# A decoder layer on one core: attention scores computed twice, the first batch in plain fp32, loads on two queues

## The reference

```python
q = silu(x @ Wq1 @ Wq2);  a = exp(log_sigmoid(sigmoid(x @ Wk1 @ Wk2)));  v = x @ Wv      # 512 channels
h[t] = a[t] * h[t-1] + (1 - a[t]) * v[t]                                                 # scan over tokens
x = layernorm(x + (rmsnorm(q * h) * norm_w) @ Wo)
# cross attention, 8 heads of 32 rows: a head is 32 rows of x and 32 rows of ctx
qk = einsum('bdm,bdn->bmn', xh, ctxh) / sqrt(32);  sm = softmax(qk, axis=-1)
x = layernorm(x + einsum('bmn,bcn->bcm', sm, ctxh))
x = layernorm(x + (silu(x @ w_gate.T) * (x @ w_up.T)) @ w_down.T)                         # hidden size 1024
```

## Time and profile before

| | us |
|---|---|
| median of 3 runs | 172.75 (172.38 to 174.07) |
| profiled execution, whole | 172.81 |
| its span on the core | 171.0 |
| PE, PEld busy | 154.1, 142.0 |
| DVE, ACT, POOL busy | 117.2, 111.9, 79.6 |
| shares of the chain that ended last | PE 70%, POOL 10%, issue 4%, ACT 4%, DMA 4%, DVE 3% |

### The profile page before, as it was taken

One profiled execution on the slowest core, in us unless ns is written; L12 is line 12 of the kernel. 1 busy time (PEld: TensorE's weight loads), 2 busy tenths in 40 slices (PEclk: granted clock), 3 DMA queues, 4 the chain that ended last, 5 costly groups with the idle time before them and its releaser, 6 DMA issues.

```text
span 171.0 us, 4005 instructions
## 1 busy us (share of the span) xinstructions
PE 154.1 (90%) x1528; PEld 142.0 (83%) x1528; DVE 117.2 (69%) x214; ACT 111.9 (65%) x258; POOL 79.6 (47%) x95
## 2 busy tenths in 40 slices
PE   7999784599987999999999999999999999899950
PEld 2799674498985899999799999979999979799940
DVE  2568887945987949786795779849749086536642
ACT  3697999859999878299776764854738860124400
POOL 1219999968975384225067123735100455016301
PEclk9999999569999999999999999999999999999995
DMA  5999960100002200000010000100020000000011
GB/s 162 312 395 402 401 230 7 59 4 0 4 0 61 67 0 4 0 0 4 2 61 4 0 6 0 61 4 0 0 64 1 2 4 0 0 0 4 0 61 61
DMA packets 5138, 10.47 MB, mean 61 GB/s; under 512 B 640, under 2 KB 1664, under 8 KB 5120
## 3 DMA queue, kind: packets, MB, share of 16 engines
q1 hardware_dynamic: 5120, 10.23, 17.1%
HBM read 9.18 MB, written 1.05 MB: 60 GB/s over the span
## 4 chain that ended last, share of the span: by engine, by line
PE 70%; POOL 10%; issue 4%; ACT 4%; DMA 4%; DVE 3%; SPq 2%; POOLq 0%; DVEq 0%; ACTq 0%
PE banks L379 38%; PE banks L523 9%; PE banks L463 7%; PE banks L529 4%; PE banks L485 4%; PE banks L450 4%; DMA ctx_raw<-ctx 4%; ACT numer L631 2%; POOL ctx_h_lo L889 2%; POOL xt_lo L923 1%; POOL w_gate_lo L907 1%; POOL o_lo L914 1%; PE banks L473 1%; PE banks L425 1%; PE banks L495 1%
## 5 line engine op out<-in xcount | busy, mean ns | idle before, releaser
L956 POOL TENSOR_TENSOR g_lo<-gu,g_hi 128x512 fp32r<-128x512 f32 x15 | 19.9, 1337 | 34.4 <-ACT g_hi L673 34.4
L631 ACT ACTIVATE numer<-banks,neg_top 128x256 f32<-128x256 f32 x64 | 29.5, 482 | 6.6 <-DVE neg_top L804 6.4
L804 DVE TENSOR_REDUCE neg_top<-banks 128x4 f32<-128x1024 f32 x16 | 19.1, 1217 | 12.0 <-PE banks L450 12.0
L665 ACT ACTIVATE gu<-banks 128x512 f32<-128x512 f32 x16 | 9.6, 598 | 19.4 <-PE banks L379 18.0
L836 DVE SCALAR_TENSOR_TENSOR gu<-gu,banks 128x512 f32<-128x512 f32 x16 | 10.9, 680 | 13.2 <-ACT gu L665 13.2
L642 ACT ACTIVATE prob<-banks 128x1024 f32<-128x1024 f32 x16 | 15.7, 1022 | 4.5 <-PE banks L463 4.4
L937 POOL TENSOR_SCALAR ve<-mv 128x2 f32<-128x2 f32 x12 | 2.3, 193 | 31.0 <-DVE mv L769 30.9
L523 PE MATMUL banks<-w_down_hi,g_hi 128*128 128x256 f32 x64 | 16.0, 284 | 0.0
L775 DVE TENSOR_SCALAR res<-banks,mv,rstd 128x256 f32<-128x256 f32 x24 | 11.9, 536 | 5.9 <-POOL rstd L939 5.8
L463 PE MATMUL banks<-ident,numer 128*128 128x128 f32 x128 | 15.8, 273 | 0.1
L523 PE MATMUL banks<-w_down_lo,g_hi 128*128 128x256 f32 x64 | 15.7, 279 | 0.0
(11 more groups left out here) (111 smaller groups left out, 456.2 us busy)
## 6 DMA issues: line engine op xcount, KB each, us to landing
prob<-w_ffn SPq DMA_DIRECT2D x4, 512.0 KB, 11.6
res<-xT SPq DMA_DIRECT2D x4, 256.0 KB, 5.5
ctx_raw<-ctx SPq DMA_DIRECT2D x4, 256.0 KB, 6.9
ctx_t<-ctxT SPq DMA_DIRECT2D x4, 256.0 KB, 4.9
res<-x SPq DMA_DIRECT2D x4, 256.0 KB, 6.4
...
```

The costliest lines, as they stand in the source:

```text
L631: ins = nc.scalar.activation(numer[:, n % 2, 2 * h + c, :], place["scores", b, i][:, 2 * h + c, :], ACT.Exp, bias=neg_top[:, 2 * i + h, c: ...
L665: nc.scalar.activation(gu[:, n % 2, :].rearrange("p (k t) -> p k t", k=2), place["hidden", b, i][:, 0:2, :], ACT.Tanh, scale=0.5).then_inc ...
L804: nc.vector.tensor_reduce(neg_top[:, 2 * i:2 * i + 2, :].rearrange("p h c -> p (h c)"), place["scores", b, i][:, :, :], AX_X, ALU.max, neg ...
L956: nc.gpsimd.tensor_tensor(g[1][:, 2 * i:2 * i + 2, :], gu[:, n % 2, :].rearrange("p (k t) -> p k t", k=2), g[0][:, 2 * i:2 * i + 2, :], AL ...
```

## The change

Six things change.

1. **Scores made twice.** The first `scores` serve the maximum alone. The maxima are rounded to fp32r, a high part and a rest next to each other (`split_top`, DVE), turned by two 128-column products for a row tile (`turn_top`) and copied by ACT (`keep_top`). PE then makes the scores again with the operands changed over, so that they come out turned, and adds the negated maxima with one more product for each head and piece (`shifted`, with `pick`). One exp of 1024 elements for two heads writes `prob` straight away (ACT). The row sums come from products with ones (`sums`, shaped as `context`), and DVE turns, inverts and spreads them with its own 32 by 32 transposes (`invert`). `turn_exp`, `inverse`, `widen` and the accumulator reads are gone. The factor of the scores moves from x1 into the exp.
2. **The first batch unsplit.** For batch 0 (`WHOLE = 1`) low, value, decay, query, mixed and both passes of scores multiply plain fp32 operands, one matmul in place of three (`whole`). x, low, the outputs, x1 and ctx of batch 0 are not split. The weights still are, for batches 1 to 3. Since the raw weights are read by batch 0, the loads that overwrite them wait for those products.
3. **Two queues.** ACT issues the loads of w_v and of the first xT, in this order, before its first activation; SP issues the others, w_high for decay and w_low first.
4. `norm1` and `norm2` are applied by ACT (a scale and a bias; POOL works out the bias with two more small steps). `norm3` stays on DVE.
5. Gate and up of a `hidden` step lie in banks of their own, each freed by its own reader.
6. The last batch's `down`, `add_down`, `norm3` and store go by halves of 128 rows, and `down` waits for both parts of the last g before its last eight and four products.

Both tables are new. There are three warm-up products in place of four.

```diff
-WARM_UP = 4
+WARM_UP = 3
 ATT_SCALE = float(D) ** -0.5
+WHOLE = 1
...
-    "sp.w_high": [[2.2, 2.7]],
...
+    "sp.w_high": [[0.7, 4.7]],
...
+    "act.load_w_v": [[0.7]],
+    "act.load_xt": [[1.2]],
...
-    "down": [[5], [0], [2], [3]],
...
+    "turn_top": [[3, 2], [0, 0], [0, 3], [4, 6]],
...
+                    "squares": [sq_turned], "mixed": [normed[0]], "sums": [sums_turned], "context": [normed[1]],
                     "turn_x": [x2_lo]}
         place, before, held = {}, {}, {}
...
             def load_ffn(c):
                 if c >= 2:
                     sp.wait_ge([low_w_lo, high_w_lo, v_w_lo, o_w_lo][c - 2], 2 if c == 3 else 1)
+                    if WHOLE:
+                        sp.wait_ge([low_done, query_done, value_done, mixed_done][c - 2], WHOLE if c == 5 else 2 * WHOLE)
                 sp.dma_start(ffn_raw[c], w_ffn[:, c, :]).then_inc(in_ffn[c], 16)
...
+            def whole(dst, weights, moving, terms):
+
+                for n, term in enumerate(terms):
+                    ins = nc.tensor.matmul(dst, weights(term), moving(term), start=(n == 0), stop=(n == len(terms) - 1))
+                return ins
...
             def low_proj(b, i):
                 ps = place["low", b, i]
                 w = 1 - i
+                if b < WHOLE:
+                    pe.wait_ge(in_low, 16)
+                    pe.wait_ge(in_xt[b], 16)
+                    whole(ps[:, 0, :], lambda c: low_raw[:, (w * EC + c) * HD:(w * EC + c + 1) * HD], xt_whole(b),
+                          range(EC)).then_inc(low_done, 1)
+                    return
                 pe.wait_ge(low_w_hi, 1)
...
             def scores(b, t):
 
                 slot = b % 2
-                pe.wait_ge(ctx_lo, b + 1)
-                pe.wait_ge(x1_lo, b + 1)
+                if b < WHOLE:
+                    pe.wait_ge(in_ctx[slot], 16)
+                    pe.wait_ge(normed[0], b + 1)
+                    for c in range(EC):
+                        for j in range(Q):
+                            ps = place["scores", b, 2 * t + j // 2]
+                            rows = slice(j * D, (j + 1) * D)
+                            ins = nc.tensor.matmul(ps[:, EC * (j % 2) + c, :], res[rows, b, t, c * P:(c + 1) * P],
+                                                   ctx_raw[rows, slot, t, :], start=True, stop=True)
+                    ins.then_inc(scores_done, 1)
+                    return
+                pe.wait_ge(ctx_lo, b + 1 - WHOLE)
+                pe.wait_ge(x1_lo, b + 1 - WHOLE)
                 for c in range(EC):
...
+            def turn_top(b, t):
+
+                pe.wait_ge(const_r, 3)
+                pe.wait_ge(top_lo, TT * b + t + 1)
+                for c in range(EC):
+                    ins = nc.tensor.matmul(ps[:, 0, c * P:(c + 1) * P], top_cols[:, t, c, :, :].rearrange("p j d -> p (j d)"), ident_r[:, :],
+                                           start=(c == 0), stop=True, skip_group_check=True)
+                ins.then_inc(top_turned, 1)
+
...
+            def shifted(b, t):
+
+                slot = b % 2
+                pe.wait_ge(top_kept, TT * b + t + 1)
+                for c in range(EC):
+                    for j in range(Q if b < WHOLE else 0):
+                        ps = place["shifted", b, 2 * t + j // 2]
+                        rows = slice(j * D, (j + 1) * D)
+                        nc.tensor.matmul(ps[:, EC * (j % 2) + c, :], ctx_raw[rows, slot, t, c * P:(c + 1) * P], res[rows, b, t, :],
+                                         start=True, stop=False)
+                    for xn, cn in ((0, 0), (0, 1), (1, 0)) if b >= WHOLE else ():
+                        for j in range(Q):
+                            ps = place["shifted", b, 2 * t + j // 2]
+                            rows = slice(j * D, (j + 1) * D)
+                            nc.tensor.matmul(ps[:, EC * (j % 2) + c, :], ctx_h[cn][rows, slot, t, c * P:(c + 1) * P],
+                                             x1_h[xn][rows, slot, t, :], start=(xn + cn == 0), stop=False)
+                    for j in range(Q):
+                        ps = place["shifted", b, 2 * t + j // 2]
+                        rows = slice(j * D, (j + 1) * D)
+                        ins = nc.tensor.matmul(ps[:, EC * (j % 2) + c, :], pick[rows, :], top_rows[rows, t, :],
+                                               start=False, stop=True)
+                ins.then_inc(shifted_done, 1)
...
+            def sums(b, i):
+
+                ps = place["sums", b, i]
+                pe.wait_ge(ones_set, 1)
                 for t in range(TT):
                     for c in range(EC):
+                        for j in range(Q):
+                            ins = nc.tensor.matmul(ps[j * D:(j + 1) * D, 0, :], ones_of[:, t, :], prob[:, Q * t + j, c, :],
+                                                   start=(t + c == 0), stop=(t + c == TT + EC - 2))
+                ins.then_inc(sums_done, 1)
...
                     pe.wait_ge(g_hi, FP * b + pair_ + 1)
+                    if last and pair_ == FP - 1:
+                        pe.wait_ge(g_lo, FP * b + pair_ + 1)
+                        for t in range(TT):
+                            high(pair_, t)
+                            rest(pair_, t).then_inc(down_done, 1)
+                        return
...
+            def load_xt(b, i):
+                act.dma_start(xt_raw[:, 0, :], xT[0]).then_inc(in_xt[0], 16)
+
+            def load_w_v(b, i):
+                act.dma_start(raw[2], wv).then_inc(in_v, 16)
...
+                if b < WHOLE:
+                    return
...
+            def keep_top(b, t):
+                act.wait_ge(top_turned, TT * b + t + 1)
+                if b >= 1:
+                    act.wait_ge(shifted_done, TT * (b - 1) + t + 1)
+                nc.scalar.activation(top_rows[:, t, :], place["turn_top", b, t][:, 0, :], ACT.Copy).then_inc(top_kept, 1)
+
             def exp(b, i):
 
-                        ins = nc.scalar.activation(numer[:, n % 2, 2 * h + c, :], place["scores", b, i][:, 2 * h + c, :], ACT.Exp,
-                                                   bias=neg_top[:, 2 * i + h, c:c + 1],
-                ins.then_inc(exp_done, 1)
-            def keep_inverse(b, i):
-                act.wait_ge(inv_turned, b + 1)
...
+
+            def norm_apply(n, b, tile):
+
+                act.wait_ge(shift_turned[n], b + 1)
+                for t in range(TT):
+                    ins = nc.scalar.activation(res[:, b, t, :], tile[:, t, :], ACT.Identity, bias=shift[:, n, t:t + 1],
+                                               scale=rstd[:, n, t:t + 1])
+                ins.then_inc(normed[n], 1)
...
+            def split_top(b, t):
+
+                whole = neg_top[:, t, :, :].rearrange("p j c -> p c j")
+                dve.wait_ge(top_done, HP * b + 2 * t + 2)
+                if b == 0:
+                    dve.wait_ge(const_r, 3)
+                if b >= 1:
+                    dve.wait_ge(top_turned, TT * (b - 1) + t + 1)
+                nc.vector.tensor_copy(top_cols[:, t, :, :, 0], whole).then_inc(top_hi, 1)
+                dve.wait_ge(top_hi, TT * b + t + 1)
+                nc.vector.tensor_tensor(top_cols[:, t, :, :, 1], whole, top_cols[:, t, :, :, 0], ALU.subtract).then_inc(top_lo, 1)
+
...
-                if b >= 1:
-                    dve.wait_ge(inv_widened, b)
-                nc.vector.reciprocal(inv[:, :, :, :], total[:, :, :, :]).then_inc(inv_done, 1)
+
+                dve.wait_ge(sums_done, b + 1)
+                nc.vector.transpose(sums_t[:, :, :].rearrange("p k d -> p (k d)"),
+                                    place["sums", b, 0][:, 0, :]).then_inc(sums_turned, 1)
+                dve.wait_ge(sums_turned, b + 1)
...
+                dve.wait_ge(inv_done, b + 1)
+                nc.vector.transpose(inv_b[:, :, :].rearrange("p t (k d) -> p (t k) d", d=D),
+                                    inv[:, :, :].rearrange("p t k -> p (t k)").unsqueeze(2).to_broadcast([P, TT * H, D])).then_inc(inv_spread, 1)
...
+                if b == B - 1:
+                    nc.vector.scalar_tensor_tensor(out=total_[:, i, :], in0=total_[:, i, :], scalar=0.5,
+                                                   in1=res[:, b, i, :], op0=ALU.mult, op1=ALU.add).then_inc(added[2], 1)
...
+                pool.wait_ge(rstd_done[n], b + 1)
+                nc.gpsimd.tensor_tensor(shift[:, n, :], mv[:, n, :, 0], rstd[:, n, :], ALU.mult).then_inc(shift_done[n], 1)
+                pool.wait_ge(shift_done[n], b + 1)
+                nc.gpsimd.tensor_scalar(shift[:, n, :], shift[:, n, :], -1.0, 0.0, ALU.mult, ALU.add).then_inc(shift_turned[n], 1)
```

501 lines of the change are left out of this document (275 added, 226 removed).

## The result

The changed kernel takes 175.89 us (median of 4 runs, 175.55 to 176.26) beside 172.8: ratio 1.0167, 95% interval 1.0109 to 1.0224. The forecast was 170.2 us in a range of 166.2 to 174.6, so both its sign and its range were wrong.

The account below looks back on a forecast made before the run. PE was taken to bound the kernel from 53.60 us to 164.67, with gaps before. PE work +4.0, start +0.3, idle time and clock -6.0 and tail -0.9 sum to -2.6: 172.81 to 170.2 us, range 166.2 to 174.6.

Parts of the forecast that it names:

- The start (+0.3): First loads: PE's first products begin at 5.2 us, where they began at 4.86, costing +0.3 us.
- Rival B: First loads come late: start at 6.7, another 1 us of low clock, 172.7 us, no change; chance 0.2.
- three readings: First loads' arrival: 5.1 us at 400 GB/s, 6.5 to 7 at the queue's later rates, 4.0 if w_v comes last.
- The idle time (-6.0): PE's gaps and lost clock, mostly before 53.6 us: 6.5 us left in place of 12.5, -6.0 (-9 to -1).
- The list of gaps: PE's remaining idle time and lost clock, counted from the start through batch 0 to the last FFN: 6.5 us.
- PE's work (+4.0): PE work removed, -16.4 us, against turn_top, shifted, sums and batch 0's plain products added: +4.0 (+2.5 to +10).
- The tail (-0.9): After PE's end: last batch by halves saves some 0.4 before the last norm and 0.5 in it, -0.9 us.
- Gate and up in single banks: Hidden steps: a bank is freed 0.7 us earlier, but PE has no such wait after 53.6 us, so 0.
- the signs: Profile checks: first scores at 30 to 32 us, ACT busy some 75, PE's end 162.5 to 163.5, tail 5.4.
- A: All gaps close: start at 4.0 to 4.9, idle term -8.5, giving 166.9 us; chance 0.22.
- C: Attention's new round trips show as PE waits for top_rows or prob over 4 us: 175.9 us; chance 0.13.
- D: Batch 0's unsplit scores don't run side by side: +10, 180 us; chance 0.05.

Follow-up runs that it names:

- 1: Changed kernel with the four first loads reversed on both queues, xT0 ahead of w_v and w_low ahead of w_high0: 173.27 us, ratio 1.0008.
- 3: Kernel before the change, given the changed kernel's order of first loads on two queues: 176.19 us, ratio 1.0181.
- 10: Changed kernel with reversed loads, GpSimd's waits for top_lo and early low_lo of batch 2, plus bank pairs of batch 0's first shifted scores exchanged: 172.76 us.
- 5: Changed kernel with reversed first loads, GpSimd also waiting for top_lo before weight pieces 6 and 10: 171.35 us, ratio 0.9909.
- 6: Changed kernel with its own load order and only GpSimd's two waits for top_lo added: 173.6 us, ratio 1.005.
- 13: Changed kernel with reversed first loads and the first batch split into high and low parts again, places not tuned: 179.19 us, ratio 1.0378.
- 14: Changed kernel with reversed loads and GpSimd's waits for top_lo, last batch's rows finished and stored whole again: 172.6 us, ratio 0.9996.

## Why the prediction was wrong

*The start (+0.3) is the first of the two steps that failed.* It was +2.5 us, with 1.75 of clock lost behind it (1.4 was in the idle term). I let 1.28 MB go ahead of the first product, at 400 GB/s from 1.9 us. The first window has 248 GB/s over 7.32 us, so 1.8 MB had moved: the two xT loads of 256 KB each that SyncE issued behind w_low, at 1.63 us, ran beside xT0, which stood second on the other queue and landed at 7.18. The rates of the first 9 us, in slices of 0.225 us:

```profile
GB/s 0 0 0 0 0 0 0 64 9 73 27 191 319 355 382 328 364 364 355 373 373 337 355 410 410 401 373 392 428 401 382 421 403 330 493 382 419 437 328 510
```

Rival B had this start (6.7) and 2.5 us for it; kernels 1 and 3 measure 2.6 and 3.3. Alone it would have given the 172.7 of B. B's size was right and its reason was not: it let the rate sag after 3.4 us, and the slices from 2.7 us to the landing stand at 319 to 428. By these slices 1.28 MB are through at some 5.95 us, 0.85 later than I assumed, because the full rate comes at 2.7 and not at 1.9; the other 1.2 us are the half MB more. I took the most hopeful of three readings, and none of the three counted the bytes behind w_low.

*The idle time (-6.0), the second, was -3.75.* The list of gaps held the wait for a bank behind an exponential (1.2, measured 1.28 and shown by 10), the ones behind `turn_top` (0.56 and two more like it) and the 0.8 ahead of the last FFN. Two of its gaps did not come, 0.8 at `squares` and 0.6 ahead of the first scores: PE is busy for all of the 22.19 us up to there. It did not hold the chain maximum, split, turn behind the second scores: the maximum takes 2.36 us for two, PE has 2.9 us of work under it (some at the low clock), and with `split_top` at 1.75 us in place of 0.36 it waits 1.47. I gave `split_top` no price at all. Nor did I count on a low clock after 10 us, and 3.49 us of it lose 1.7. These two, 1.47 and 1.7, with 0.35 more of clock at the start and without the 1.4 that did not come, are the miss but for 0.1. Taking GpSimd's hold on `split_top` away won 1.9 to 2.3 us (5 and 6). Of that 1 us is the wait; the rest is clock, which falls behind these gaps in some runs and not in others, and that the hold makes it fall is not shown. That the mechanism was in sight (x_h_lo, 128x512, took from 0.63 to 1.64 us in the kernel before) I saw only afterwards.

*PE's work (+4.0) was +5.6*, right in its mechanism, short in its terms. Plain products take 0.452 us (two records of 0.226) for 0.43: +0.6 over 28. I had set the 0.45 that the warm-up gave aside as the start of an empty array, and it was the steady value. The unsplit scores take 1.12 to 1.15 a tile for 0.9, +0.4, and the unsplit `shifted` 1.3 for 1.15, +0.3; another 0.3 is the clock of the second eight records. The steady `shifted` and `sums` measure as forecast, so that making the scores twice buys PE nothing. These four come to the 1.6 us. The +5.6 is a remainder, though, and smaller terms of either sign in it are not settled.

*The tail (-0.9)* was right: -1.1 in the trace, -1.2 when taken out (-1.0 in the span). *Gate and up in single banks* was not tried alone; PE has no wait there.

*A slip and the signs.* The 0.9 us lost to the clock in the kernel before does not follow from the numbers beside it: 10 matmuls at 0.118 are 1.18 of 1.83 us, which leaves 0.65 (the timeline has only eight that start in that stretch, and with eight it is 0.9). Of the signs, ACT was to be busy for 75 us and is for 89.2, PE was to end at 162.5 to 163.5 and ends at 168.96, and the first scores were to start at 30 to 32 and start at 33.19; ACT's miss is not in PE's waits and I did not follow it up.

*The rivals.* A assumed a start before 4.9; with that start and no hold on `split_top` (5) the kernel stands at 171.35, not at 166.9: the round trips of batch 0 don't all find cover, and PE's work is 1.6 us over. C gave the right time, 175.9, by luck: PE's waits for top_rows and for the exponentials sum to 2.5 us, and over 4 would have been needed. Its mechanism is there in part, since the 1.47 us for top_cols, which its sign left out, are a round trip too. D is out (1.15 us for 16 records side by side).

With the two costs gone the change gives 171.35 us, 1.2 above the forecast and 1.6 below the kernel before, which is at the edge of what can be told. What pays in it is the unsplit first batch (at most 5.9 us by 13) and the halves (1.2 us by 14). The scores made twice, with the norms and banks that come along, were not tried alone. Taking both numbers at their word they would cost more than they bring, but 13 was not tuned, so this is not shown.
